# Swapping the order of two waits at three places of a step-by-step recurrence on VectorE

## The chip, the cores and the metric

The kernel runs on one core of a Trainium2 chip. The metric is the device time of one launch in microseconds, as the median of several runs. TensorE (PE in the rows) multiplies matrices, VectorE (DVE) and ScalarE (ACT) do elementwise work, GpSimd (POOL) and the DMA queues move and prepare data. The engines run independent instruction streams and wait for each other through semaphores.

## What is computed

A stack of four layers, each with an attention-like part and a feed-forward part. The change touches only the attention part of the first layer, a recurrence over the 256 tokens of each of 16 sequences:

```python
def step(M, kv):
    k_t, v_t = kv
    v_pred = jnp.einsum('bf,bfd->bd', k_t, M)
    surprise = jnp.linalg.norm(v_t - v_pred, axis=-1, keepdims=True)
    delta = k_t[:, :, None] * v_t[:, None, :]
    M = M + eta_c[None, :, None] * surprise[:, :, None] * delta
    return (_ln2(M), None)          # mean and variance over the whole matrix M
M, _ = jax.lax.scan(step, M0, (kT, vT))
```

Each step needs a norm (one square root) of the step before, and a normalization (a second square root). Every step hangs on the one before it.

## The kernel before, in words

The program is one long list of stages with a barrier between them. Stage 4 is the recurrence. It does not carry the matrix M from token to token. It takes chunks of C = 8 tokens (32 chunks, counted from 0 like the steps): TensorE works out the products between the tokens of a chunk once, and inside the chunk only scalars per sequence are carried, as columns of 128 partitions.

In a chunk, `scan_dve` first runs a head (`head_dve`, with TensorE in a ping-pong of products, then L983 to L988), and then eight steps `t`. One step works as follows.

- L1010 (in the last part of the step before; for the first step L984) writes `zv`, the negated square of the norm, and signals `sc_z`.
- ScalarE waits for it (L839) and takes the first root, L840: `Wst[:, t]`, the step's weight; it signals `sc_w`.
- L1001, on VectorE, makes `X2` from the weight and signals `sc_x`. It has two waits: L993 for VectorE's own step counter `dv` (the result of L968, `ahead_dve`), and L994 for `sc_w`. In the last step of a chunk L996 takes its place.
- ScalarE waits for `sc_x` (L841) and takes the second root, L842: `Pv`, the new standard deviation; it signals `sc_r`. Behind that it does a scaling of a part of the state matrix (steps 0 to 2) or a copy out of PSUM (steps 3 to 6).
- VectorE meanwhile updates the table `D` (L1002, 7 x 10 columns in the first step and fewer in each later one), then `YE` (L1005, with waits L1003 for `dv` and L1004 for `sc_x`), then `D`'s last column (L1007).
- L1010 writes the next `zv`, with waits L1008 for `dv` (the result `YE`) and L1009 for `sc_r`. Then come L1012 (`ahead_dve`, L967), L1013 (`CE`) and L1016 (`start_dve`, L972), which waits for L1013's result.

VectorE takes its instructions in the order in which they are written. `e.wait_ge(sem, n)` puts a wait ahead of the next operation. `stt` is the helper at L225, so the profile shows all these operations on L225, and ScalarE's roots on L213.

Of the kernel before, what the change touches and what calls it, by code (L numbers as in the profile page):

```python
# [132 lines left out]
def program(nc, xT, early, wts, bia, con, m1, m2, m3, outT):  # L133
    with ExitStack() as ctx:
# [13 lines left out]
        def signals(engine, *counts):  # L148
            out = []
            for n in counts:  # L150
                s, base = idle[engine].pop(0) if idle[engine] else (sem(f"{engine}_{next(made)}"), 0)
                out.append(Signal(s, base))
                held.append((engine, s, base + n))
            return out
# [61 lines left out]
        def tt(e, out, a, b, op):  # L216
            return e.tensor_tensor(out, a, b, op)  # L217
# [6 lines left out]
        def stt(e, out, a, s, b, op0, op1):  # L224
            return e.scalar_tensor_tensor(out=out, in0=a, scalar=s, in1=b, op0=op0, op1=op1)  # L225
# [7 lines left out]
        def cp(e, out, a):  # L233
            return e.tensor_copy(out, a)
# [476 lines left out]
        def tables_sp(e):  # L711
# [35 lines left out]
        sc_base, sc_sq, sc_w, sc_r, sc_rcc, sc_scl, sc_new = signals(  # L747
            "scalar", 30, 31, 256, 256, 31, 248, 124)
        sc_zero, = signals("gpsimd", 2)
        sc_vw, sc_wc, sc_xm, sc_ex, sc_rp, sc_vwr, sc_x, sc_z, sc_pT, sc_m, sc_last = signals(  # L750
            "vector", 32, 32, 31, 31, 32, 32, 256, 256, 62, 8, 32)
# [131 lines left out]
        def moved_dve(e, c, a):  # L883
            e.wait_ge(*sc_up(8 * (c - 1) + 4 + a // 2 + 1))
            e.wait_ge(*sc_new(4 * (c - 1)))
            stt(e, Mst[:, a, :], Mst[:, a, :], Rc[:, a:a + 1], moved(a), MU, AD).then_inc(sc_m.sem, 1)

        def weights_dve(e, dn, c):

            ttr(e, tmp8, Wst, one8_, wown).then_inc(dv, 1); e.wait_ge(dv, dn.up())  # L890
            ts(e, vw, VTOK[:, c - 1, :], wown, None, MU).then_inc(sc_vw.sem, 1)
            tt(e, wc, wown, CN[:, c - 1:c], MU).then_inc(sc_wc.sem, 1)

        def scaled_dve(e, dn, c):

            if c > 1:
                e.wait_ge(*sc_up(8 * (c - 1)))
            ts(e, wcr, wc, rR, None, MU).then_inc(dv, 1); dn.up()
            e.wait_ge(*sc_vw(c))
            ts(e, vwr, vw, rR, None, MU).then_inc(sc_vwr.sem, 1)  # L900

        def tail_dve(e, dn, c):

            e.wait_ge(*sc_r(8 * c))
            e.reciprocal(rR, Pv).then_inc(dv, 1); e.wait_ge(dv, dn.up())
            if c > 1:
                e.wait_ge(*sc_rc(c - 1))
            ts(e, rp8, K("pairm"), rR, None, MU).then_inc(sc_rp.sem, 1)
            tt(e, rr, rR, rR, MU).then_inc(dv, 1); dn.up()
# [38 lines left out]
        def cross_dve(e, c):  # L948
            e.wait_ge(*sc_cross(c))
            tt(e, XMK[c % 2].rearrange("p (k n) -> p k n", k=4), PS[:, 0, :].rearrange("p (k n) -> p k n", k=4),  # L950
               K("blk").rearrange("p (k n) -> p k n", k=1).broadcast_to((128, 4, 128)), MU).then_inc(sc_xm.sem, 1)

        def pairs_dve(e, dn, c):

            T_ = RT[c % RTB]
            e.wait_ge(s_rt[c % RTB], 16 * (c // RTB) + 16)
            cp(e, C2[:, :, 0], T_[:, :, 81]).then_inc(dv, 1); dn.up()
            tt(e, C2[:, 0:7, 1], T_[:, 1:8, 80], T_[:, 0:7, 81], MU).then_inc(dv, 1); e.wait_ge(dv, dn.up())
            tt(e, C2[:, 0:7, 1], C2[:, 0:7, 1], T_[:, 1:8, :].rearrange("p j x -> p (j x)")[:, 0:6 * (TX + 11) + 1:TX + 11], AD).then_inc(dv, 1)
            e.wait_ge(dv, dn.up())  # L960

        def twice(ap):
            return ap.rearrange("p (r x) -> p r x", x=2) if ap.shape[1] == 4 else ap.rearrange("p (r x) -> p r x", r=1).broadcast_to((128, 2, 2))

        def ahead_dve(e, dn, T_, t):

            stt(e, D[:, t, 10:11], D[:, t, 9:10], T_[:, t + 1, 80:81], D[:, t + 1, t:t + 1], MU, AD).then_inc(dv, 1)  # L967
            return dn.up()  # L968

        def start_dve(e, dn, T_, t):  # L970

            stt(e, CE[:, 1:2], CE[:, 0:1], T_[:, t + 1, 80:81], D[:, t + 1, 11:12], MU, AD).then_inc(dv, 1)  # L972
            return dn.up()

        def scan_dve(e, dn):
            pairs_dve(e, dn, 0)
            for c in range(NC):
                T_ = RT[c % RTB]
                if c:
                    head_dve(e, dn, c)  # L980

                D0 = PS[:, 7, 0:96].rearrange("p (j x) -> p j x", x=12) if c else D
                tt(e, YE[:, 1:2], T_[:, 0, 80:81], D0[:, 0, 11:12], AD).then_inc(dv, 1); e.wait_ge(dv, dn.up())  # L983
                tt(e, zv, D0[:, 0, 8:9], YE[:, 1:2], MN).then_inc(sc_z.sem, 1)  # L984
                if c:
                    cp(e, Dall, PS[:, 7, 0:96]).then_inc(dv, 1); e.wait_ge(dv, dn.up())
                n_A = ahead_dve(e, dn, T_, 0)
                n_E = start_dve(e, dn, T_, 0)  # L988
                if c == 0:
                    cross_dve(e, 1)  # L990
                for t in range(C):
                    w_ = Wst[:, t:t + 1]
                    e.wait_ge(dv, n_A)  # L993
                    e.wait_ge(*sc_w(8 * c + t + 1))  # L994
                    if t == C - 1:
                        stt(e, X2[:, 0:1], C2[:, t, 0:1], w_, D[:, t, 9:10], MU, AD).then_inc(sc_x.sem, 1)  # L996
                        weights_dve(e, dn, c + 1)
                        e.wait_ge(*sc_x(8 * c + t + 1))
                        stt(e, qv, X2[:, 0:1], w_, qv, MU, AD).then_inc(sc_last.sem, 1)
                        break  # L1000
                    stt(e, twice(X2), twice(C2[:, t, 0:2]), w_, twice(D[:, t, 9:11]), MU, AD).then_inc(sc_x.sem, 1)  # L1001
                    stt(e, D[:, t + 1:8, t:10], T_[:, t + 1:8, 11 * t:10 * t + 10], w_, D[:, t + 1:8, t:10], MU, AD).then_inc(dv, 1); n_D = dn.up()  # L1002
                    e.wait_ge(dv, n_E)  # L1003
                    e.wait_ge(*sc_x(8 * c + t + 1))  # L1004
                    stt(e, YE[:, 0:4], X2, w_, CE, MU, AD).then_inc(dv, 1); n_Y = dn.up()  # L1005
                    e.wait_ge(dv, n_D)
                    stt(e, D[:, t + 1:8, 11], D[:, t + 1:8, t], w_, D[:, t + 1:8, 11], MU, AD).then_inc(dv, 1); n_F = dn.up()  # L1007
                    e.wait_ge(dv, n_Y)  # L1008
                    e.wait_ge(*sc_r(8 * c + t + 1))  # L1009
                    stt(e, zv, D[:, t + 1, 8:9], Pv, YE[:, 1:2], MU, MN).then_inc(sc_z.sem, 1)  # L1010
                    if t + 2 < C:
                        n_A = ahead_dve(e, dn, T_, t + 1)  # L1012
                    stt(e, CE[:, 0:3:2], YE[:, 0:5:4], 1e-5, YE[:, 2:3].broadcast_to((128, 2)), MU, AD).then_inc(dv, 1); n_E = dn.up()  # L1013
                    if t + 2 < C:
                        e.wait_ge(dv, n_E)
                        n_E = start_dve(e, dn, T_, t + 1)  # L1016
            tail_dve(e, dn, NC)
            scaled_dve(e, dn, NC)
            e.wait_ge(*sc_rc(NC))
            cp(e, Rc, PS[:, 4, 256:264]).then_inc(dv, 1); e.wait_ge(dv, dn.up())  # L1020
            for a in range(8):
                moved_dve(e, NC, a)
# [1936 lines left out]
        def _(e):  # L2959
# [6 lines left out]
            first_dve(e, dn)  # L2966
            barrier(e, st.up())
            scan_dve(e, dn)
            barrier(e, st.up())
            mo_dve(e)  # L2970
# [154 lines left out]
```

## Time and profile before

| | us |
|---|---|
| median of the runs | 2213.94 |
| fastest and slowest run | 2213.69 and 2222.31 |
| the profiled execution's own span | 2256.3 |
| VectorE busy in it | 1357.7 (60%) |
| TensorE busy in it | 1912.8 (85%) |
| ScalarE busy in it | 1044.8 (46%) |

The span is of one profiled execution. A row of a timeline has the start, the duration, the engine, the line, the operation, and what it writes and reads, with sizes in partitions x columns. Behind that stands in brackets for how long the engine was idle and what ended this. DVEq is VectorE's instruction queue: what stands there is handled by the queue and is not work of the engine.

### The profile page before, as it was taken

To read this page: it belongs to the slowest core of one execution; us is meant where nothing else is said; L and a number is where in the kernel's file an instruction comes from. 1 tells how busy PE (TensorE), PEld (TensorE's weight loads), DVE (VectorE), ACT (ScalarE), POOL (GpSimd) and SP (SyncE) were. 2 spreads that over 40 slices of the span, in tenths; PEclk is the share of its full clock that TensorE was granted. 3 is DMA by queue.
4 is the path that set the end of the run, shared out by engine and by line. 5 is a ranking of instruction groups with operands and counts; after the bars stand their busy time and mean duration, and the time that the engine had idled before them with its cause. 6 is when DMAs were issued, how large, how long until landed. Compare 5 with 4: busy or idle time off the path is not lost.

```text
span 2256.3 us, 35340 instructions
## 1 busy us (share of the span) xinstructions
PE 1912.8 (85%) x12022; PEld 1293.6 (57%) x12022; DVE 1357.7 (60%) x4960; ACT 1044.8 (46%) x2490; POOL 319.3 (14%) x455
## 2 busy tenths in 40 slices
PE   6887777787778799999999888888899954999888
PEld 4464566666666566886555776555454542973333
DVE  3777888888888644676333485542121431569886
ACT  2433555665566423333444223454344313437667
POOL 0001000000000000330000002003126023406642
PEclk9999666667676568898999657998999967988989
DMA  2001100000000000000001100003013200635662
GB/s 111 1 13 36 32 22 22 19 19 25 19 19 19 34 1 1 2 3 2 0 1 75 40 1 1 1 15 97 13 12 50 89 14 30 113 69 91 98 103 40
DMA packets 93282, 76.09 MB, mean 34 GB/s; under 512 B 22320, under 2 KB 85168, under 8 KB 92336
## 3 DMA queue, kind: packets, MB, share of 16 engines
q1 hardware_dynamic: 85424, 65.31, 12.8%
q0 software_dynamic: 7680, 8.53, 2.0%
q8 instruction: 97, 1.59, 0.3%
q14 instruction: 81, 0.66, 0.1%
HBM read 48.86 MB, written 23.51 MB: 32 GB/s over the span
## 4 chain that ended last, share of the span: by engine, by line
PE 56%; DVE 23%; ACT 6%; DMA 4%; issue 4%; SPq 3%; another core or an unknown queue 1%; POOL 1%; DVEq 0%; PEld 0%; PEldq 0%; ACTq 0%; POOLq 0%
PE ps L204 52%; DVE sm L225 8%; ACT big L213 3%; DVE mw L225 3%; DMA d_pt<-big 3%; DVE big L217 2%; PE ps L208 2%; PE ps L2465 2%; SPq L2552 1%; DVE big L231 1%; DVE tmp L221 1%; ACT sm L213 1%; SPq L866 1%; DVE big L225 1%
## 5 line engine op out<-in xcount | busy, mean ns | idle before, releaser
L213 ACT ACTIVATE tmp<-ps,bi 128x512 f32<-128x512 f32 (+1 forms) x226 | 153.9, 684 | 200.8 <-PE ps L204 189.3
L204 PE MATMUL ps<-big,mw 128*128 128x512 f32 (+3 forms) x476 | 236.3, 593 | 11.6 <-DVEq L252 5.6
L213 ACT ACTIVATE sm<-sm 128x1 f32<-128x1 f32 x512 | 174.4, 341 | 106.6 <-DVE sm L225 96.0
L204 PE MATMUL ps<-ke,big 32*128 32x128 f32 (+2 forms) x1632 | 154.0, 296 | 62.3 <-ACT big L212 61.8
L204 PE MATMUL ps<-big,co 128*128 128x256 f32 (+1 forms) x360 | 180.5, 636 | 27.9 <-DMA bi<-bia 12.2
L213 ACT ACTIVATE big<-ps,co 128x512 f32<-128x512 f32 (+1 forms) x296 | 174.5, 648 | 61.3 <-PE ps L204 58.2
L204 PEld LDWEIGHTS ps<-ke,big 32*128 32x128 f32 (+2 forms) x1632 | 132.3, 195 | 87.4 <-ACT big L212 72.0
L231 DVE TENSOR_REDUCE big<-ps 128x2 f32<-128x512 f32 x256 | 161.2, 675 | 21.0 <-PE ps L204 20.7
L204 PE MATMUL ps<-ke 48*128 48x256 bf16 (+4 forms) x638 | 127.5, 315 | 34.7 <-DVE big L217 16.7
L204 PE MATMUL ps<-big,tmp 128*32 128x256 f32 (+2 forms) x1180 | 137.5, 424 | 22.9 <-DVE tmp L221 17.6
L217 POOL TENSOR_TENSOR big<-big,co 128x512 f32<-128x512 f32 x32 | 40.1, 1274 | 765.6 <-ACT big L212 765.6
L204 PE MATMUL ps<-tmp,mw 128*128 128x512 f32 x288 | 140.9, 601 | 0.7 <-ACT tmp L212 0.7
L204 PE MATMUL ps<-big 128*32 128x128 f32 (+5 forms) x898 | 130.1, 299 | 10.3 <-DMA big<-big 5.1
L204 PE MATMUL ps<-big,wt 128*128 128x512 f32 x208 | 114.5, 653 | 24.8 <-DVEq L252 14.4
L204 PEld LDWEIGHTS ps<-big,co 128*128 128x128 f32 x360 | 88.9, 276 | 75.8 <-issue 27.1
L204 PEld LDWEIGHTS ps<-co,sm 128*128 128x128 f32 (+1 forms) x708 | 95.2, 208 | 64.4 <-DVE sm L333 37.6
L212 ACT ACTIVATE big<-ps 128x256 f32<-128x256 f32 (+4 forms) x244 | 90.7, 381 | 89.2 <-PE ps L204 72.6
L204 PEld LDWEIGHTS ps<-big,mw 128*128 128x128 f32 (+1 forms) x476 | 93.0, 229 | 66.5 <-issue 36.8
L204 PE MATMUL ps<-co,sm 128*128 128x128 f32 (+1 forms) x708 | 109.1, 304 | 22.6 <-DVE sm L333 12.6
L204 PEld LDWEIGHTS ps<-ke 128*128 128x128 f32 (+3 forms) x638 | 65.9, 133 | 92.4 <-DVE big L217 23.5
L225 DVE SCALAR_TENSOR_TENSOR sm<-sm,mw 128x1 f32<-128x1 f32 (+1 forms) x480 | 101.0, 221 | 23.3 <-ACT sm L213 13.0
L204 PE MATMUL ps<-tmp,wt 128*128 128x512 f32 (+1 forms) x212 | 102.5, 574 | 11.6 <-issue 5.8
(254 smaller groups left out, 3834.5 us busy)
## 6 DMA issues: line engine op xcount, KB each, us to landing
mw<-d_tab SPq DMA_DIRECT2D x32, 328.0 KB, 3.4
mw<-m SPq DMA_DIRECT2D x2, 4096.0 KB, 12.7
d_pt<-big SPq DMA_DIRECT2D x32, 192.0 KB
ke<-d_pt SPq DMA_DIRECT2D x72, 64.0 KB
big<-d_pt SPq DMA_DIRECT2D x72, 64.0 KB
mw<-d_pt SPq DMA_DIRECT2D x48, 64.0 KB
d_xs<-big SPq DMA_DIRECT2D x1, 2560.0 KB, 15.3
big<-d_xs SPq DMA_DIRECT2D x5, 512.0 KB, 6.4
```

Source lines behind the costliest of these rows:

```text
L204: return e.matmul(out, lhsT, rhs, start=start, stop=stop)
L208: return e.transpose(out, a, K("ident")[0:n, 0:n])
L212: return e.activation(out, in_, f, scale=scale, **kw)
L213: return e.activation(out, in_, f, bias=K("zero")[0:out.shape[0], :] if bias is None else bias, scale=scale, **kw)
L217: return e.tensor_tensor(out, a, b, op)
L221: return e.tensor_scalar(out, a, s1, None, op0)
L225: return e.scalar_tensor_tensor(out=out, in0=a, scalar=s, in1=b, op0=op0, op1=op1)
L231: return e.tensor_reduce(out, a, AX, op)
L866: e.dma_start(BIG[2 + hh][q, :].rearrange("p (c x) -> p c x", x=256)[:, :, 64 * (b % 4):64 * (b % 4) + 64], EKT[q, 16 * hh:16 * hh + 16, : ...
L2465: p = e.matmul(o, TMP[:, 2 + i % 2, 128 * j:128 * j + 128], MW[:, bass.ds(x * 512 + (4096 + 128 * j), 128)], start=False, stop=(j == 3))
L2552: e.dma_start(st_[j][r0 + 8 * t:r0 + 8 * t + 8], d_pt[n, j, part].rearrange("(h d) n -> d h n", d=8)).then_inc(s_st[n % 4], 16)
```

## The change

At three places of a step, the two waits ahead of an operation are written in the other order. Nothing else differs.

```diff
                 for t in range(C):
                     w_ = Wst[:, t:t + 1]
+                    e.wait_ge(*sc_w(8 * c + t + 1))
                     e.wait_ge(dv, n_A)
-                    e.wait_ge(*sc_w(8 * c + t + 1))
                     if t == C - 1:
                         stt(e, X2[:, 0:1], C2[:, t, 0:1], w_, D[:, t, 9:10], MU, AD).then_inc(sc_x.sem, 1)
...
+                    e.wait_ge(*sc_x(8 * c + t + 1))
                     e.wait_ge(dv, n_E)
-                    e.wait_ge(*sc_x(8 * c + t + 1))
                     stt(e, YE[:, 0:4], X2, w_, CE, MU, AD).then_inc(dv, 1); n_Y = dn.up()
...
+                    e.wait_ge(*sc_r(8 * c + t + 1))
                     e.wait_ge(dv, n_Y)
-                    e.wait_ge(*sc_r(8 * c + t + 1))
                     stt(e, zv, D[:, t + 1, 8:9], Pv, YE[:, 1:2], MU, MN).then_inc(sc_z.sem, 1)
```

## Rows read from the trace of the kernel before

**Rows 1.** The page: span, and the chain that ended last by engine.

```profile
span 2256.3 us, 35340 instructions
...
PE 56%; DVE 23%; ACT 6%; DMA 4%; issue 4%; SPq 3%; another core or an unknown queue 1%; POOL 1%; DVEq 0%; PEld 0%; PEldq 0%; ACTq 0%; POOLq 0%
```

**Rows 2.** Busy time by stretches: PE, PEld, DVE, ACT, POOL; clock, DMA share, GB/s.

```profile
215.00:775.00 560.00, 428.42 (x2494) 354.18 (x2494) 478.38 (x2870) 330.01 (x977) 5.30 (x2) 0.67 0.08 22
```

**Rows 3.** Groups of ScalarE, 215 to 775: count, busy us, mean ns, idle before.

```profile
L213 ACT ACTIVATE sm<-sm 128x1 f32<-128x1 f32 x512 | 174.4, 341 | 106.6 <-DVE sm L225 96.0
```

**Rows 4.** Timeline around step 5 of chunk 10: start, duration, engine, operation.

```profile
401.50 0.22 DVE L225 SCALAR_TENSOR_TENSOR sm<-mw,sm 128x1 f32<-128x1 f32 x1
...
401.75 0.30 ACT L213 ACTIVATE sm<-sm 128x1 f32<-128x1 f32 x1
...
401.96 0.22 DVE L225 SCALAR_TENSOR_TENSOR sm<-sm,mw 128x1 f32<-128x1 f32 x1
...
402.41 0.39 ACT L213 ACTIVATE sm<-sm 128x1 f32<-128x1 f32 x1 [0.36 <-DVE sm L225]
402.48 0.22 DVE L225 SCALAR_TENSOR_TENSOR sm<-sm 128x4 f32<-128x4 f32 x1
...
402.70 0.36 ACT L212 ACTIVATE big<-ps 128x256 f32<-128x256 f32 x1
...
402.90 0.22 DVE L225 SCALAR_TENSOR_TENSOR sm<-mw,sm 128x1 f32<-128x1 f32 x1
```

**Rows 5.** The chain of waits in that step: start, duration, what.

```profile
402.15 0.22 DVE sm L225
...
402.84 0.02 DVEq L1009
402.86 0.04 issue
```

**Rows 6.** Instructions of VectorE's queue by line: count, ns min/median/max, first and last.

```profile
L994 DVEq EVENT_SEMAPHORE  x256: 21/21/21, 222.6 to 769.2; - x128
...
L1009 DVEq EVENT_SEMAPHORE  x224: 21/21/21, 223.4 to 768.6; - x112
```

**Rows 7.** Timelines of two normalization stages: ScalarE's root, then VectorE's operation.

```profile
801.81 0.26 ACT L213 ACTIVATE sm<-ps,co 128x4 f32<-128x4 f32 x1 [0.38 <-PE ps L204]
802.11 0.17 DVE L221 TENSOR_SCALAR sm<-sm 128x4 f32<-128x4 f32 x1 [1.43 <-ACT sm L213]
...
862.22 0.27 ACT L213 ACTIVATE sm<-ps,co 128x4 f32<-128x4 f32 x1 [1.00 <-PE ps L204]
862.51 0.17 DVE L221 TENSOR_SCALAR sm<-sm 128x4 f32<-128x4 f32 x1 [0.57 <-ACT sm L213]
```

**Rows 8.** Timeline, end of chunk 10: second root, L999's operation and the reciprocal.

```profile
405.27 0.39 ACT L213 ACTIVATE sm<-sm 128x1 f32<-128x1 f32 x1 [0.36 <-DVE sm L225]
...
405.63 0.21 DVE L225 SCALAR_TENSOR_TENSOR sm<-sm 128x1 f32<-128x1 f32 x1
405.76 0.15 DVE L905 RECIPROCAL sm<-sm 128x1 f32<-128x1 f32 x1
```

**Rows 9.** Timeline, first step of chunk 11, and the scalings ahead of it.

```profile
411.45 0.87 ACT L213 ACTIVATE big<-big,co,sm 128x128 f32<-128x128 f32 x2
...
412.61 0.22 DVE L225 SCALAR_TENSOR_TENSOR sm<-sm,mw 128x4 f32<-128x4 f32 x1
412.75 0.28 DVE L225 SCALAR_TENSOR_TENSOR mw<-mw,sm 128x70 f32<-128x70 f32 x1
412.95 0.22 DVE L225 SCALAR_TENSOR_TENSOR sm<-sm 128x4 f32<-128x4 f32 x1
413.08 0.23 DVE L225 SCALAR_TENSOR_TENSOR mw<-mw,sm 128x7 f32<-128x7 f32 x1
...
413.16 0.48 ACT L213 ACTIVATE big<-big,co,sm 128x128 f32<-128x128 f32 x1
...
413.36 0.22 DVE L225 SCALAR_TENSOR_TENSOR sm<-mw,sm 128x1 f32<-128x1 f32 x1
```

**Rows 10.** Stretches from last `X2` to next `zv`, chunks 1 and 10; columns as rows 2.

```profile
250.15:255.92 5.77, 3.88 (x27) 3.23 (x30) 5.19 (x33) 2.93 (x9) 0.00 (x0) 0.89 0.20 60
405.02:411.78 6.76, 5.57 (x26) 4.92 (x29) 5.45 (x32) 2.74 (x8) 0.00 (x0) 0.50 0.18 52
```

**Rows 11.** The stretch from 1265 to 1374; columns as rows 2.

```profile
1265.00:1374.00 109.00, 97.03 (x346) 76.11 (x346) 72.80 (x352) 28.41 (x121) 0.00 (x0) 0.50 0.09 21
```

## The prediction

> **What bounds the kernel now.** I read the page's head first: the profiled execution spans 2256.3 us, and its chain of work names TensorE for 56% and VectorE for 23% [rows 1]. Then the table by stretches, to find where VectorE could be the limit: the recurrence fills about 560 us, from 215 to 775, with VectorE busy 478.38 of them and TensorE at a granted clock of 0.67 [rows 2]. The groups of instructions of that stretch show 512 tiny ScalarE operations on one column, 341 ns each [rows 3]: two square roots for each of 256 steps (32 chunks of 8).
>
> The timeline of one step gives the loop [rows 4]. The root's operand `zv` is made at 401.50 (0.22 us, L1010). ScalarE takes the first root (L840) from 401.75 to 402.05. `X2` (L1001) starts at 402.15, which the chain shows on its own [rows 5]. ScalarE takes the second root (L842) from 402.41 to 402.80. The next `zv` starts at 402.90. So a step is 1.40 us, all of it in this loop: 0.22 + 0.03 + 0.30 + 0.10 + 0.22 + 0.04 + 0.39 + 0.10. The two gaps of 0.10 are the way from ScalarE back to VectorE. In the second, the chain has an instruction of VectorE's queue on L1009, 0.02 long, at 402.84, 0.04 behind the root's end and 0.06 ahead of the operation that it lets go [rows 5]. The chain puts the time before it on VectorE's L225, which ends there by chance: in the first step of a chunk the last such operation ends at 413.31 and `zv` starts at 413.36 [rows 9], less than those 0.06 later, so the root is what released it.
>
> **Which wait stands where.** An operation carries one wait; a second becomes an instruction of its own ahead of it. Of the two written at L993 and L994, the trace has a record for L994 alone, 256 of them, and of L1008 and L1009 for L1009 alone, 224 [rows 6]. So the wait written second stands alone, and the one written first is carried. Before, the root's signal stands alone and `dv`, fulfilled long ago, is carried. The change turns this round at L994, L1004 and L1009. It adds and removes no instruction, no bytes and no wait.
>
> **What a carried signal costs.** Of this loop the trace does not show it, so I bound it by neighbours. In normalization stages a VectorE operation that carries ScalarE's signal itself, with the engine idle, starts 0.02 us after the root's end (862.49 to 862.51) and 0.04 after (802.07 to 802.11) [rows 7]. These have the same engines, the same function and also a handful of columns, so I take their middle, 0.03. The other end is today's 0.10, no gain. A carried wait gains 0.07 per handover.
>
> **The sum, place by place**, with times counted from the operation named.
>
> L1009, `zv` (7 in a chunk). It wants the root's end: `X2` + 0.22 + 0.04 + 0.39 = 0.65, and with 0.03 it starts at 0.68, today 0.75. Now `YE` is what the standalone instruction waits for. Its slowest case is the first step, where `YE` stands 0.34 behind `X2` because the widest `D` (70 columns) is ahead of it, and takes 0.22 [rows 9]: 0.56, plus the 0.10 of a standalone wait, 0.66. That is 0.02 ahead of 0.68; narrower steps have more room, 0.33 today at [rows 4] and earlier afterwards. Gain 0.07 each.
>
> L994, `X2`. In the first and the last step of a chunk nothing is close in front of it on VectorE: 0.07 each. In the six between, the start of the next sum (L972, 401.96) hangs on `zv` alone, 0.46 behind it. Two neighbours on this engine start 0.14 apart (`X2` at 412.61, `D` at 412.75 [rows 9]), so `X2` can't start before 0.60; the root would let it go at 0.22 + 0.03 + 0.30 + 0.03 = 0.58. Today it is 0.65 (402.15 less 401.50). The gain is cut to between 0.05 and 0.06. What is late next there is that L972 operation. The new standalone wait, for L968's result of the same step, is behind L972 in the queue; L972 is let go at 401.96 and the wait needs 0.06, 402.02, before the 402.10 at which `X2` starts.
>
> L1004, `YE`. Its own signal from `X2` comes up to 0.06 sooner, and `YE` off the path gains 0 to 0.07 that goes to L1009's cover. In the sum: nothing. If that cover were gone, `zv` would lose at most what `YE` is late; nothing queues behind these waits but the operations of the same step.
>
> ScalarE has to follow. Behind the second root it does a scaling or a copy, 0.29 later (402.70 [rows 4]), and two scalings back to back start 0.39 apart (0.87 for two, one taking 0.48 [rows 9]). The next first root can start 0.68 behind the second one; the loop wants it at 0.39 + 0.03 + 0.22 + 0.03 = 0.67. The 0.01 disappears in the 0.02 by which L972 holds `X2` anyway.
>
> Per chunk: 7 x 0.07 + 2 x 0.07 + 6 x 0.055 = 0.96 us; over 32 chunks 30.7 us. The part between the last `X2` and the next chunk's first `zv` (405.02 to 411.78, TensorE ping-pong) has none of the three waits and moves along unchanged. Against its own time the profiled execution goes from 2256.3 to 2225.6. The plain runs have a median of 2213.94, 42 us under that span; a handover in nanoseconds is the same there as far as any row tells, so I take the whole: 2213.9 - 30.7 = 2183.
>
> A rule speaks against it. The Trainium skill, "VectorE: DVE Perf Modes", section "The DRAIN you can't avoid", says that the next VectorE operation does not start until the pipe of the one before has emptied. By it `X2` couldn't start before L972's end. The trace disagrees already: L972 ends at 401.96 + 0.22 = 402.18 and `X2` starts at 402.15 [rows 4, 5].
>
> **Rivals.**
> (a) A held engine: a VectorE operation that goes by a carried signal starts only once its predecessor is through. Then `X2` starts in six steps of eight at 0.46 + 0.22 = 0.68 instead of 0.60: 6 x 0.08 x 32 = 15.4 us of the gain go, 2199. Against: the reciprocal L905 carries the second root's signal of 405.66, and starts at 405.76 while its neighbour runs until 405.84 [rows 8]. 5%. The rule above would have the same effect.
> (b) Recording is part of the 0.10. The 42 us between span and median must lie somewhere; if the recorded standalone instructions hold a good part, a plain handover costs perhaps 0.065 and only half is won: 2199. No row speaks for it or excludes it. 9%.
> (c) The change doesn't do what it says, because which wait is carried goes by something else than the order: 2214. Against it both lines of [rows 6]. 4%.
> (d) The clock turns it into a loss. Place: the stages after the recurrence, where TensorE is busy almost throughout and everything now comes 31 us sooner against the chip's changes of clock. From 1265 to 1374 the granted clock is 0.50, its 1.2 GHz level, with TensorE busy for 97.03 of 109 us [rows 11]; at the upper level that work would take as little as half, so one more such stretch costs up to 48.5 us: 2232. It decides from about 62 us more at the low level. For it, such a stretch exists; against it, the runs of the kernel before lie within 9 us. 3%.
> (e) The clock helps: the part between chunks took 6.76 us at clock 0.50 and once 5.77 us at 0.89 [rows 10]. Denser chunks may keep it up in more of the 31: if in ten, 10 us more, 2173. 5%.
>
> **How the numbers follow.** Forecast 2183 with 74%; its own spread is the hop of 0.02 to 0.04 (480 handovers x 0.01 = 5 us either way) and the 9 us between runs. (a) to (e) as above. Leaving out (c), (d) and the far side of (e), the range is 2172 to 2200. A difference of 0.5% (11 us, under 2203 or over 2225) is about what a measurement here can tell from none. Faster: forecast, (a), (b), (e), 93%, less 1 for a gain that falls short: 92%. Same: (c) and that 1%: 5%. Slower: (d), 3%.
>
> **What would show it.** In the changed kernel's profile: steps of 1.27 us between starts of `zv`, ScalarE's root ending 0.03 ahead of both `X2` (first and last step) and `zv`; 0.05 ahead of `X2` between; the standalone instructions early, none between root and operation; the recurrence about 31 us shorter, other stages equal. (a) shows as `X2` 0.68 behind `zv`; (b) as 1.27 steps in the profile with a small gain in the plain runs; (c) as steps of 1.40. The sum is wrong if another operation sets a step that I have with 0.02 of room: the first step's `YE`, or L972.

## The result, and the profile after

The changed kernel takes 2177.84 us (median of 4 runs, 2173.17 to 2185.62), the kernel before 2214.28 in the same comparison (4 runs, 2213.69 to 2222.31). The ratio is 0.9834, 95% interval 0.981 to 0.9858: 36.4 us less, where 30.7 were forecast, and 2178 where 2183 was forecast. The page of the profile after, its span and its chain by engine, answers to [rows 1]:

```profile
span 2183.8 us, 35340 instructions
PE 58%; DVE 17%; ACT 15%; issue 3%; DMA 3%; SPq 2%; POOL 1%; PEld 0%; DVEq 0%; PEldq 0%; ACTq 0%; POOLq 0%
```

VectorE has 17% of the chain now, 23% before [rows 1]: with the operation itself carrying the root's signal, the stretch from the root's end to the operation is given to ScalarE and to "issue". The 512 roots cost what they did (mean of one 339 ns, 341 in [rows 3]).

VectorE's queue has its standalone instructions of the first place on L994 as before, 256 of them, but L994 is now the wait on `dv` (columns as [rows 6]):

```profile
L994 DVEq EVENT_SEMAPHORE  x256: 21/21/21, 225.3 to 739.5; - x128
```

The timeline of step 5 of chunk 10 after the change, the same step as [rows 4]. It can be read from `zv` to `zv` as there:

```profile
395.87 0.22 DVE L225 SCALAR_TENSOR_TENSOR sm<-mw,sm 128x1 f32<-128x1 f32 x1
396.12 0.29 ACT L213 ACTIVATE sm<-sm 128x1 f32<-128x1 f32 x1
396.33 0.35 DVE L225 SCALAR_TENSOR_TENSOR sm<-sm,mw 128x1 f32<-128x1 f32 x2
396.60 0.22 DVE L225 SCALAR_TENSOR_TENSOR mw<-mw,sm 128x10 f32<-128x10 f32 x1
396.72 0.39 ACT L213 ACTIVATE sm<-sm 128x1 f32<-128x1 f32 x1 [0.30 <-DVE sm L225]
396.74 0.22 DVE L225 SCALAR_TENSOR_TENSOR sm<-sm 128x4 f32<-128x4 f32 x1
397.13 0.22 DVE L225 SCALAR_TENSOR_TENSOR sm<-mw,sm 128x1 f32<-128x1 f32 x1
```

`zv` starts at 395.87 and again at 397.13: 1.26 us (median of all such steps 1.267; 1.400 before). The second root ends at 396.72 + 0.39 = 397.11, and `zv` starts at 397.13. The timeline draws `X2` together with the operation ahead of it ("x2" at 396.33), so its start is read in the chain of waits:

```profile
396.12 0.30 ACT sm L213
396.43 0.04 issue
396.46 0.23 DVE sm L225
```

`X2` starts at 396.46, 0.04 behind the root, where it was 0.10 [rows 4, 5]. `YE`, at 396.74, is 0.28 behind `X2` instead of 0.33. No instruction of the queue (DVEq) is on this path any more.

Over all 32 chunks, counted in the trace from the first `zv` to the last `X2`: 548.5 us before (220.78 to 769.28), 515.1 after (224.93 to 740.08), 33.4 less. Of these, 28.7 are between the first and the last `zv` of the chunks (321.1 to 292.4), 2.6 are the last steps, from `zv` to `X2` (21.2 to 18.6: 32 x 0.07, and 0.4 of a single last step, in chunk 22, that took 1.02 us before), and 2.1 are the parts between chunks (206.2 to 204.1). The same work by engine, before and then after (columns as [rows 2]):

```profile
220.78:769.28 548.50, 425.80 (x2460) 351.88 (x2460) 471.27 (x2847) 329.62 (x976) 0.00 (x0) 0.67 0.07 21
224.93:740.08 515.15, 405.97 (x2460) 340.81 (x2460) 450.76 (x2847) 321.79 (x976) 0.00 (x0) 0.69 0.08 22
```

The mean granted clock of the recurrence went from 0.67 to 0.69, and TensorE is busy 20 us less with the same 2460 matmuls. In the steps the loop runs between VectorE and ScalarE, so little of this can show in the time.

The two profiled spans differ by far more, 2256.3 less 2183.8 = 72.5 us. Two stages where experts' weights are read by DMA hold half of it: counted from barrier to barrier, one is 72.4 us long before and 58.5 after, the other 46.4 and 23.7. The second one, by stretches (columns as [rows 2]), in the profile of before

```profile
1850.00:1897.00 47.00, 29.82 (x96) 17.28 (x96) 5.35 (x9) 10.79 (x16) 27.84 (x29) 0.69 0.12 42
```

and in that of after:

```profile
1805.00:1829.00 24.00, 23.56 (x96) 14.60 (x96) 5.14 (x9) 10.99 (x16) 18.21 (x20) 0.89 0.15 53
```

The same 96 matmuls take 47 and 24 us, at a clock of 0.69 and of 0.89, with 42 and 53 GB/s moved. Together the two stages are 37 us shorter, the recurrence 33.4, the last stage 4.2, the rest about 2 longer. Whether the 37 us belong to the change is what the fourth run below asks.

### The profile page after: what moved, and what is told of

Same layout as the page of the kernel before. It is cut to its first block, busy times and chain, and to the rows that moved or that the text cites. A ratio compares the mean times of both kernels' runs of the same rounds, so it can differ in the third digit from the quotient of the medians.

```text
span 2183.8 us, 35340 instructions
## 1 busy us (share of the span) xinstructions
PE 1879.7 (86%) x12022; PEld 1280.4 (59%) x12022; DVE 1335.5 (61%) x4960; ACT 1035.1 (47%) x2490; POOL 318.6 (15%) x455
## 4 chain that ended last, share of the span: by engine, by line
PE 58%; DVE 17%; ACT 15%; issue 3%; DMA 3%; SPq 2%; POOL 1%; PEld 0%; DVEq 0%; PEldq 0%; ACTq 0%; POOLq 0%
PE ps L204 54%; ACT sm L213 7%; ACT big L213 5%; DVE big L231 3%; DVE sm L225 3%; DVE big L217 3%; PE ps L208 2%; PE ps L2465 2%; ACT big L212 2%; DMA d_pt<-big 2%; DVE tmp L221 1%; SPq L866 1%; DVE big L225 1%; DVE sm L221 1%; DMA mw<-big 1%
## 5 line engine op out<-in xcount | busy, mean ns | idle before, releaser
L204 PE MATMUL ps<-big,co 128*128 128x256 f32 (+1 forms) x360 | 170.9, 614 | 25.8 <-DMA bi<-bia 12.3
L204 PE MATMUL ps<-ke,big 32*128 32x128 f32 (+2 forms) x1632 | 149.3, 292 | 49.3 <-ACT big L212 48.5
L204 PEld LDWEIGHTS ps<-ke,big 32*128 32x128 f32 (+2 forms) x1632 | 128.8, 191 | 73.1 <-ACT big L212 58.7
L204 PE MATMUL ps<-big,tmp 128*32 128x256 f32 (+2 forms) x1180 | 132.5, 415 | 21.3 <-DVE tmp L221 16.2
L204 PE MATMUL ps<-big,wt 128*128 128x512 f32 x208 | 109.0, 625 | 16.8 <-DVEq L252 14.3
L213 ACT ACTIVATE big<-big,co,sm 128x128 f32<-128x128 f32 x248 | 107.5, 480 | 1.0
L212 ACT ACTIVATE tmp<-ps 128x128 f32<-128x128 f32 (+2 forms) x177 | 61.9, 362 | 89.9 <-PE ps L204 52.8
## 6 DMA issues: line engine op xcount, KB each, us to landing
d_xs<-big SPq DMA_DIRECT2D x1, 2560.0 KB, 16.1
```

What stands on the lines that cost most here:

```text
L204: return e.matmul(out, lhsT, rhs, start=start, stop=stop)
L212: return e.activation(out, in_, f, scale=scale, **kw)
L213: return e.activation(out, in_, f, bias=K("zero")[0:out.shape[0], :] if bias is None else bias, scale=scale, **kw)
```

## The experiments

Each was compared with runs of the kernel before on the same chip. In what follows, "recurrence" is the time from the first `zv` to the last `X2` in the run's profile, and the gaps are medians over the steps from the end of a root to the start of the operation that it lets go.

**Each swap alone.** First the one at `X2`, against the kernel before:

```diff
-                    e.wait_ge(dv, n_A)
                     e.wait_ge(*sc_w(8 * c + t + 1))
+                    e.wait_ge(dv, n_A)
```

> Only the pair ahead of X2 (L993/L994) is swapped. Theory: each root-to-VectorE handover costs 0.10 us with the root's wait standing alone and 0.03 carried, cut to 0.05 won in the six middle steps, where the operation at L972 is close ahead. Won: 32 x (2 x 0.07 + 6 x 0.055) = 15.0 us, about 0.7%; in the profile X2 starts 0.03 behind the root in the first and last step of a chunk, 0.05 less late in the others, zv still 0.10 behind its root; step 1.34 us. Rival, the gain comes from one place only: all 36 us or none.

Measured: 2232.74 us against 2249.48, ratio 0.9935 (0.9912 to 0.9957). Recurrence 532.4, step 1.334. The second root of one step and the `zv` behind it:

```profile
403.52 0.39 ACT L213 ACTIVATE sm<-sm 128x1 f32<-128x1 f32 x1 [0.30 <-DVE sm L225]
404.01 0.22 DVE L225 SCALAR_TENSOR_TENSOR sm<-mw,sm 128x1 f32<-128x1 f32 x1
```

The second root ends at 403.91 and `zv` starts at 404.01: still 0.10. `X2` has its short gap, 0.034 in the first and last steps and 0.045 between. Then the one at `zv` alone:

```diff
-                    e.wait_ge(dv, n_Y)
                     e.wait_ge(*sc_r(8 * c + t + 1))
+                    e.wait_ge(dv, n_Y)
```

> Only the pair ahead of zv (L1008/L1009) is swapped. Theory: 7 x 32 x 0.07 = 15.7 us won, about 0.7%, zv 0.03 behind its root, X2 0.10 behind its; step 1.33 us. If the gains of this and of the swap at X2 add up to that of the whole change, the two handovers are independent terms of one sum; if the sum exceeds the whole, L972 or YE has become the limit more often than the profile says.

Measured: 2234.50 us, 0.9946 (0.9912 to 0.9981). Recurrence 535.9, step 1.331:

```profile
398.78 0.39 ACT L213 ACTIVATE sm<-sm 128x1 f32<-128x1 f32 x1 [0.36 <-DVE sm L225]
399.20 0.22 DVE L225 SCALAR_TENSOR_TENSOR sm<-mw,sm 128x1 f32<-128x1 f32 x1
```

Now the second root (to 399.17) is followed after 0.03, and between the roots 0.36 pass instead of the 0.30 above: `X2` still has its 0.10. Between the `zv` of the chunks the one swap takes 14.2 us out, the other 14.0, both together 28.5 (all three against the profile of before on this chip; 28.7 in the first pair). So the two add up. The expectations for the whole recurrence were 15.0 and 15.7, and 16.1 and 12.7 are measured. Part of the second miss lies in the parts between chunks, which took 1.3 us longer in that run; another part is one single step, which is taken up below.

The third, at `YE`:

```diff
-                    e.wait_ge(dv, n_E)
                     e.wait_ge(*sc_x(8 * c + t + 1))
+                    e.wait_ge(dv, n_E)
```

> Only the pair ahead of YE (L1003/L1004) is swapped. Theory: YE starts up to 0.07 us sooner behind X2 and nothing else moves, since zv waits for its root, not for YE: 0 us (within 0.3%), step 1.40 us. Rival: YE is on the path, and 7 x 32 x up to 0.07 = up to 15.7 us are won.

Measured: 2245.44 us, 1.0004 (0.9979 to 1.0029). Step 1.400, as before; recurrence 546.5, 2.0 less, of which 1.2 in the parts between chunks, where nothing was edited. The chain of waits shows the start of `X2`, the timeline that of `YE`, the operation with 4 columns:

```profile
406.54 0.23 DVE sm L225
```

```profile
406.80 0.39 ACT L213 ACTIVATE sm<-sm 128x1 f32<-128x1 f32 x1 [0.36 <-DVE sm L225]
406.82 0.22 DVE L225 SCALAR_TENSOR_TENSOR sm<-sm 128x4 f32<-128x4 f32 x1
407.29 0.22 DVE L225 SCALAR_TENSOR_TENSOR sm<-mw,sm 128x1 f32<-128x1 f32 x1
```

`YE` comes 0.28 behind `X2` instead of 0.33 [rows 4, 5], and nothing follows from it, because `zv` waits for the root (to 407.19). This swap works as the others do, and is worth nothing by itself.

**The kernel before, profiled again.** No edit. It asks whether recording lengthens the run by the 42 us between span and median, and whether the two expert stages belong to the change.

> The kernel before, unchanged. The first profile of it spans 2256.3 us, 42 us over the plain runs' median. If recording a profile costs that, this span will again be about 2256. If it was that one execution, in stages far from the recurrence (the two expert stages, where the profiles of before and after differ by 13.9 and 22.7 us), the span will be near 2212 to 2222 and the recurrence (first zv to last X2) again 548 us.

Measured: 2248.72 us, 1.0 (0.997 to 1.0031), 28 runs of before on that chip with a median of 2249.48. The profiled execution was one of this kernel's runs: span 2249.8, time 2251.6. A span and 1.8 us around it are the time, so recording has no visible part in it. The recurrence took 548.55 us, within 0.1 of the first profile. The two expert stages took 71.5 and 45.1 us here. Over all the profiles of this study, whatever the kernel, they go by the chip: on the two chips where the kernel before takes 2249 and 2254 us (eight profiles) they took 69.5 to 72.4 and 43.0 to 45.2, and on those where it takes 2214 to 2217 (five profiles, all of changed kernels) 58.5 to 58.7 and 23.3 to 24.0. The first profile of before has the long ones, 72.4 and 46.4. So these 37 us go with the chip and not with the change, and they answer to the 35 us between the two levels. That the unchanged kernel has the short ones on a chip of the second kind was not profiled, and what makes them longer was not tried.

**More conditions behind the root's wait, and ahead of it.** If the price is that of a standalone instruction that comes after the signal, more of it must cost more, and a condition that is put ahead of it must cost nothing. First, the kernel before with two fulfilled conditions more at each of the two operations:

```diff
                     e.wait_ge(dv, n_A)
+                    e.wait_ge(*sc_z(8 * c + t + 1))
                     e.wait_ge(*sc_w(8 * c + t + 1))
+                    e.wait_ge(s_tw, 64)
...
                     e.wait_ge(dv, n_Y)
+                    e.wait_ge(*sc_x(8 * c + t + 1))
                     e.wait_ge(*sc_r(8 * c + t + 1))
+                    e.wait_ge(*sc_w(8 * c + t + 1))
```

> The kernel before, with two more waits, long fulfilled, written at X2 and at zv, so that between the standalone wait for the root and the operation stands a second standalone instruction. Theory: what costs is each instruction that VectorE's queue must still take after the signal. The 0.10 is 0.04 to the wait, and 0.06 from there to the operation; one more adds between its own 0.02 and 0.06: a gap of 0.12 to 0.16 at both roots, 480 handovers, 10 to 29 us slower. Rival: the 0.07 is a fixed price of a wait of that kind, paid once: gap 0.10, no difference.

Measured: 2316.70 us (two runs) against 2254.01, 1.0282 (1.0179 to 1.0385); recurrence 601.2, step 1.595. Both gaps are 0.200. The queue's instructions at the first place, and the chain through both places of one step:

```profile
L995 DVEq EVENT_SEMAPHORE  x256: 21/21/21, 222.8 to 822.0; - x128
L996 DVEq EVENT_SEMAPHORE  x256: 49/50/50, 222.8 to 822.0; - x128
```

```profile
402.48 0.05 DVEq L996
402.53 0.04 issue
402.57 0.22 DVE sm L225
...
403.25 0.02 DVEq L1012
403.27 0.05 issue
403.32 0.05 DVEq L1013
403.37 0.04 issue
403.42 0.22 DVE sm L225
```

One standalone instruction is 0.021 long and another 0.050. The one that I added takes up two conditions, not one, and with its way to the engine it adds 0.10 at each root, so the recurrence gets 52.7 us longer. The direction is as expected and the size is not: the expectation was for 10 to 29 us. What a second standalone instruction with one condition costs was not run. The place of the price is shown: behind the root's end comes the root's own standalone instruction (L995, L1012), then 0.04 to 0.05, then the next, then the operation.

The other way round, the changed kernel with one fulfilled condition more at each place, written after the one on `dv`:

```diff
                     e.wait_ge(dv, n_A)
+                    e.wait_ge(*sc_z(8 * c + t + 1))
...
                     e.wait_ge(dv, n_Y)
+                    e.wait_ge(*sc_x(8 * c + t + 1))
```

> The changed kernel, with one more fulfilled condition written at X2 and at zv. It joins the standalone instruction ahead of the operation, which carries the root's wait. Theory: what is handled before the signal comes is free: X2 and zv 0.03 to 0.05 behind their roots, step 1.27 us, same time as the changed kernel. Rival, the number of conditions is what costs: step longer by 0.02 or more.

Measured: 2228.08 us against 2254.01, 0.9873 (0.9804 to 0.9942); step 1.267, gaps 0.034 and 0.045, recurrence 516.8. Conditions written behind the root's wait (two of them, in one instruction) cost 0.10 at a root; one written ahead of the operation's own signal costs nothing that can be read.

**What holds `X2` at 0.045.** The prediction put it on the start of the next sum (L972). That operation waits for the new `CE`; here `CE` is written ahead of `ahead_dve`, so L972 is let go sooner (on top of the changed kernel):

```diff
-                    if t + 2 < C:
-                        n_A = ahead_dve(e, dn, T_, t + 1)
                     stt(e, CE[:, 0:3:2], YE[:, 0:5:4], 1e-5, YE[:, 2:3].broadcast_to((128, 2)), MU, AD).then_inc(dv, 1); n_E = dn.up()
                     if t + 2 < C:
+                        n_A = ahead_dve(e, dn, T_, t + 1)
                         e.wait_ge(dv, n_E)
```

> The changed kernel, with CE's operation (L1013) written ahead of ahead_dve's (L1012). The operation at L972 waits for CE and can then start at 0.14 + 0.16 + 0.04 = 0.34 behind zv by its data, and at 0.14 + 0.13 + 0.14 = 0.41 by its neighbours, not at 0.46. Theory: L972 is what holds X2 0.01 in six steps of eight; without that X2 waits for nothing but its root (gap 0.03 and not 0.045) unless the standalone wait, now for a result that comes at 0.27 + 0.22 = 0.49 and through the queue 0.10 later at 0.59, holds it at the same place: 0 to 2 us won in the recurrence, step 1.255 to 1.27. Rival: the gap of 0.045 in the middle steps has nothing to do with L972 and stays when L972 is gone from in front of it.

Measured: 2220.26 us (two runs), 0.9854 (0.979 to 0.9918); recurrence 514.9. `X2` now starts 0.033 behind the root in every step, 0.582 behind `zv` (0.594 in the changed kernel), and a step is 1.261. In the timeline, the operation on 2 columns is `CE`, and the row "x2" is L972's operation, at 388.99, with `X2` behind it; the chain then gives `X2` by itself:

```profile
388.79 0.16 DVE L225 SCALAR_TENSOR_TENSOR sm<-sm 128x2 f32<-128x2 f32 x1
388.86 0.22 DVE L225 SCALAR_TENSOR_TENSOR mw<-mw 128x1 f32<-128x1 f32 x1
388.91 0.29 ACT L213 ACTIVATE sm<-sm 128x1 f32<-128x1 f32 x1
388.99 0.47 DVE L225 SCALAR_TENSOR_TENSOR sm<-sm,mw 128x1 f32<-128x1 f32 x2
```

```profile
389.24 0.04 DVE sm L225
```

The root ends at 389.20. L972 stands 0.25 ahead of `X2` now, where it stood 0.13 ahead of it in the changed kernel (396.33 and 396.46). So the limit was the operation in front, and it is worth 0.012 of a middle `X2`'s start. Only 0.006 of that reaches the step (1.267 to 1.261): the later `X2` is recorded 0.217 long and the earlier one 0.223. The edit also moves the standalone wait that stands behind L972. That wait wasn't the limit: it ends 0.10 ahead of `X2` in both kernels, while 0.04 to 0.05 pass from such an instruction to the operation that it lets go. The same kernel on a further chip:

> The same kernel as ce_first, for its time beside fifth_between on one chip. Recurrence from first zv to last X2 about 515 us, ratio to before about 0.984 on a chip where the kernel before takes 2217 us, 0.986 where it takes 2250.

Measured: 2187.61 us against 2216.61, 0.9858 (0.9825 to 0.9892); recurrence 514.6. Whole runs can't tell it from the changed kernel (0.9834), as is right for 1 us.

**The same swap in the part between chunks.** `pairs_dve` ends on a wait for `dv` and the next operation (L929) waits for TensorE; with the order turned round L929 carries TensorE's signal (on top of the last kernel):

```diff
-            pairs_dve(e, dn, c)
-            e.wait_ge(*sc_p1(c))
+            pairs_dve(e, dn, c, sc_p1(c))
...
+            if also is not None:
+                e.wait_ge(*also)
             e.wait_ge(dv, dn.up())
```

> As ce_first, and in the part between chunks one more pair of waits is turned round: the operation at L929 then carries TensorE's signal (L928), and the older wait for VectorE's own step stands alone. Theory: the same 0.07 is to be had on the way from TensorE to VectorE: L929 starts 0.07 sooner behind the product, and as TensorE waits for what follows it (pT1), the part between chunks gets up to 0.07 shorter, 31 x 0.07 = 2.2 us. Rival: another input of that part is later, and its length stays.

Measured: 2224.72 us (two runs), 0.9874 (0.9843 to 0.9906); recurrence 514.6, against 514.9 without it. The timeline of VectorE, L929's operation and the one behind it, in this kernel

```profile
400.91 0.29 DVE L217 TENSOR_TENSOR tmp<-ps,co 128x128 f32<-128x128 f32 x1 [0.21 <-PE ps L204]
401.34 0.29 DVE L217 TENSOR_TENSOR mw<-big,ps 128x128 f32<-128x128 f32 x1
```

and in the kernel before

```profile
407.26 0.29 DVE L217 TENSOR_TENSOR tmp<-ps,co 128x128 f32<-128x128 f32 x1 [0.28 <-PE ps L204]
407.62 0.29 DVE L217 TENSOR_TENSOR mw<-big,ps 128x128 f32<-128x128 f32 x1
```

In these two chunks L929 starts 2.85 behind the chunk's last `X2`, and 2.92 in the kernel before. The next, `pT1`, is 0.43 behind L929 instead of 0.36, so it starts 3.28 behind `X2` in both. Over all chunks the medians are 3.12 and 3.18 for L929 with and without this swap, and 3.55 and 3.54 for `pT1`. `pT1` waits for its own product from TensorE, and the gain is lost at once. The swap does the same thing here, and pays nothing, because another signal ends last.

**Scalings off the first root.** In the first step of a chunk ScalarE is late by the scalings put ahead of it [rows 9]: 1.431 us for this step after the change, 1.267 for the others. First, on top of the last kernel, four scalings ahead of the first root, and four behind the second roots of steps 0 to 3, which moves the copies to steps 4 to 7:

```diff
-                    for a in range(5):
+                    for a in range(4):
...
-                    if c and t < 3:
-                        scaled_act(e, 5 + t)
-                    elif c and t < 7:
-                        k = t - 3
+                    if c and t < 4:
+                        scaled_act(e, 4 + t)
+                    elif c:
+                        k = t - 4
```

> As head_swap, and with one of ScalarE's five scalings taken out of the part between chunks: four there, the fifth behind the second root of step 0, the others and the four copies one step later each. In all profiles so far the first root of a chunk starts 0.28 us behind its zv, and not 0.03, because ScalarE is still at the fifth scaling. Theory: the first root then starts when its zv is there: 31 x 0.25 = 7.7 us less than the version before it, step 0 at 1.18 instead of 1.43 us, and the last copy's followers (the products for the next chunk, and the copy of them) still end before the head needs them. Rival: they do not, since they start one step later; the part between chunks grows by up to what was won.

Measured: 2211.02 us against 2217.49, 0.9961 (0.9933 to 0.9988): most of the gain is gone. The first step is shorter, 1.364, but the part between chunks is 7.90 us instead of 6.76, and the recurrence 538.0. These parts grew by 26 us in all (231.3 against 205.0), where the rival of the expectation had at most what the first steps win. ScalarE at the end of chunk 10 in this kernel (last root at 403.31, `X2` at 403.05)

```profile
403.31 0.39 ACT L213 ACTIVATE sm<-sm 128x1 f32<-128x1 f32 x1 [0.29 <-DVE sm L225]
403.60 0.36 ACT L212 ACTIVATE big<-ps 128x256 f32<-128x256 f32 x1
405.11 0.38 ACT L212 ACTIVATE big<-ps 128x256 f32<-128x256 f32 x1 [1.15 <-PE ps L204]
406.45 0.40 ACT L213 ACTIVATE mw<-mw,co 128x128 f32<-128x128 f32 x1 [0.95 <-DVE mw L217]
```

and in the changed kernel (last root at 399.24, `X2` at 398.99)

```profile
399.24 0.39 ACT L213 ACTIVATE sm<-sm 128x1 f32<-128x1 f32 x1 [0.29 <-DVE sm L225]
399.53 0.36 ACT L212 ACTIVATE big<-ps 128x256 f32<-128x256 f32 x1
400.99 0.40 ACT L213 ACTIVATE mw<-mw,co 128x128 f32<-128x128 f32 x1 [1.09 <-DVE mw L217]
```

A copy more stands between the last root and the operation on `mw`. It waits 1.15 us for TensorE, and `mw` starts 3.14 us behind the root instead of 1.75. So a piece that is moved behind a root is free only where nothing later hangs on it.

Then the same idea without touching the copies: the fifth scaling goes between ScalarE's two roots of the first step, where it idles for 0.30 us (on top of the kernel with the two operations exchanged):

```diff
-                    for a in range(5):
+                    for a in range(4):
...
+                    if c and t == 0:
+                        scaled_act(e, 4)
```

> As ce_first, with ScalarE's fifth scaling not ahead of a chunk's first root but between its two roots, where ScalarE otherwise waits for X2; all later scalings and copies stay in their steps. In four_scalings the first root started with its zv, but X2 then followed only 0.20 behind, 0.684 behind zv: VectorE's own list (the copy of the table, L968, L972) is next. Theory: step 0 at 1.364 instead of 1.431, 31 x 0.067 = 2.1 us less in the recurrence, the part between chunks as before at 6.76 or 6.50, because the last copy is again in step 6. Rival: what made four_scalings slower was not the last copy's step, and the part between chunks again takes 7.90.

Measured: 2172.98 us against 2216.61, 0.9816 (0.9766 to 0.9866); recurrence 512.2, first step 1.364, the parts between chunks as before. The first step of chunk 10:

```profile
389.19 0.16 DVE L217 TENSOR_TENSOR sm<-ps,sm 128x1 f32<-128x1 f32 x1
389.39 0.29 ACT L213 ACTIVATE sm<-sm 128x1 f32<-128x1 f32 x1
389.59 0.48 ACT L213 ACTIVATE big<-big,co,sm 128x128 f32<-128x128 f32 x1
390.14 0.39 ACT L213 ACTIVATE sm<-sm 128x1 f32<-128x1 f32 x1
```

The first root follows its `zv` directly and the scaling fills the idle time: it ends at 390.07, and the second root, let go by `X2`, starts at 390.14. In this first step `X2` now comes 0.197 behind the root, because VectorE's own operations ahead of it (the copy of the table, L968, L972) take that long, as the expectation said. Of the kernels run this one has the shortest recurrence, 3 us under the changed kernel's; a whole run can't tell that difference.

**The changed kernel once more:**

> The changed kernel, in the same call and so on the same chip as four_scalings, and beside runs of the kernel before. Theory: 30.7 us of the sum plus up to 2 us in the parts between chunks: ratio 0.985 to 0.987, whatever the level of the chip (2214 or 2250 us before).

Measured: 2183.95 us against 2217.49, 0.9834 (0.9798 to 0.987). Recurrence 515.6, 0.5 from the first profile's 515.1. The ratio lies under the 0.985 to 0.987 that was expected, which its interval still touches.

## Why the prediction was right, step by step

**The loop and its price.** The step of 1.27 us was forecast and is 1.267. The handover, taken from two places of other stages [rows 7] as 0.03, is 0.033 at `zv` and at the first and last `X2`. This was the term on which the sum hung most, and the middle of the two neighbours came out right. The runs with one swap each show it place by place, 14.2 and 14.0 us between the `zv` of the chunks.

**The rule of the pipe.** After the change L972's operation runs from 396.33 to 396.55 (0.22 long), and `X2`, which carries the root's signal, starts at 396.46, 0.09 before that end. So this operation, which carries a signal, isn't held until its neighbour is through, and rival (a), 2199, falls. The sentence of the Trainium skill that stood beside it ("VectorE: DVE Perf Modes", section "The DRAIN you can't avoid") doesn't hold here either. The same section adds that a next operation which is not held starts earlier, which the prediction left out; the trace agrees with that addition, with `X2` 0.136 behind the start of L972.

**The limit on the middle `X2`.** The prediction said that L972 keeps `X2` from coming before 0.60 behind `zv`, and took 0.055 of the 0.07. `X2` is 0.594 behind `zv`, down from 0.652: 0.057. That it was this operation, and not something else in the queue, was argued then; the run with the two operations exchanged shows it, since the gap falls to 0.033. The step falls by 0.006 only, to 1.261. So L972's price was put too high for the step: a middle step gained 0.133, where the sum has 0.07 + 0.055 = 0.125.

**The rest of the loop.** `YE` was to gain nothing, and alone it gains nothing (1.0004). The first step's `YE` was said to have 0.02 of room: its root goes 0.033 to `zv` like all others, so it had room. ScalarE's spacing of operations was said to leave `zv` to root at 0.04 where a scaling is ahead, and 0.039 is what is measured there.

**The sum.** 0.96 us a chunk, 30.7 in all, was worked out. The places that it names gave 28.7 + 2.2 = 30.9, without the odd last step of chunk 22. That this fits to 0.2 is in part luck, since two misses of 1.5 us cancel. The middle steps gained 192 x 0.008 more than the sum has. Against that, step 4 of chunk 1 took 3.06 us where it had taken 1.64. ScalarE's copy ahead of its first root waits there for a product of TensorE, before and then after:

```profile
245.28 0.38 ACT L212 ACTIVATE big<-ps 128x256 f32<-128x256 f32 x1 [0.33 <-PE ps L204]
249.42 0.38 ACT L212 ACTIVATE big<-ps 128x256 f32<-128x256 f32 x1 [1.81 <-PE ps L204]
```

TensorE itself had waited for a DMA, which did not become faster. Its row after:

```profile
246.13 1.24 PE L204 MATMUL ps<-tmp,big 32*128 32x128 f32 x16 [3.95 <-DMA big<-big]
```

These matmuls start 21.2 us behind the recurrence's first `zv` in both kernels. The prediction had looked at what ScalarE does behind its second root, and not at what its copies wait for. With one swap alone this step took 2.33 and 2.31 us.

The other thing that the sum had wrong, by a little, is "moves along unchanged" for the parts between chunks: they took 2.1 us less in all, 31 parts of a median of 6.75 to 6.76 in both kernels, with six under 6.35 us after the change and one before. These six are the ones with a higher granted clock, 0.68 to 0.77, and the one before had 0.89 [rows 10]. The part behind chunk 11 after the change:

```profile
415.10:421.31 6.21, 4.68 (x28) 4.11 (x30) 5.37 (x32) 2.73 (x8) 0.00 (x0) 0.69 0.18 55
```

This is rival (e) on a small scale, 2 us and not 10. Recurrence as a whole: 33.4 less in the first pair of profiles, 548.6 less 515.6 = 33.0 in the second.

**Rival (b), recording.** It is refuted: a profiled execution of the kernel before takes 1.8 us more than its span and lies among the plain runs of its chip, and the short steps stand in the plain runs at full price. The 42 us between span and median, which the prediction carried along unexplained, are mostly the level of the chip, in two stages that the change doesn't touch. To take the gain off the median and leave the 42 alone was right.

**Rivals (c) and (d).** The wait written second stands alone after the change too, so (c) fell. (d) didn't come: apart from the two expert stages and the last, the 26 other stages behind the recurrence each differ by 3.1 us at most between the two first profiles, and 23 of them by 0.2 or less.

**What stays open.** The whole run gained 36.4 us (31 to 42 by the interval), the recurrence 33.4. The 3 us between are inside the spread of the runs (12 us), and no run could place them. The last stage took 233 to 251 us from profile to profile, whatever the kernel, which alone is more than these 3 us.

## What to carry to other kernels

Where an operation in a serial loop has two waits, look in the trace for which of them stands as an instruction of its own, and let that be the one that is fulfilled early; here it was worth 0.07 us at each place on the loop, and nothing at a place (`YE`, L929) where another signal ended last. Price the next thing in line before counting a saving whole: the operation in front kept 0.012 of 0.07 at the start of a middle `X2`, and a product that hung on a DMA cost 1.5 us of the gain in one step. A saving that is small per step is best read in the steps of the trace, which agreed to 0.1 us between two profiles of the kernel before while whole runs differed by some 35 us from chip to chip.

## What the runs showed of the hardware that was not expected

- A standalone wait behind the signal costs by what it holds: with one condition it is 0.021 us long, with two 0.050, and a second such instruction in a row makes the gap 0.20 us where one makes it 0.10 and none 0.033.
- Two stages with weights read by DMA took 69.5 to 72.4 and 43.0 to 46.4 us in nine profiles, 58.5 to 58.7 and 23.3 to 24.0 in five others, while a step of the recurrence was the same to 0.001 us on both (1.267).
- Small VectorE operations of 0.22 us start 0.13 to 0.14 apart and overlap at their ends (396.33 to 396.46; 396.60 to 396.74), and behind the one on 2 columns, 0.16 long, the next started after 0.07 (388.79 to 388.86).
